# A decoder block on one core: the opening in a new order, scales spread by transposes, first bit chunk high half first

## The reference, cut to what matters

```python
# 1 expert layer: two int8-like "smooth quantised" products with a silu product between
s = sqrt(max|x|, per column / max|w|, per column)
xs, ws = x / s, w * s
x_scale, w_scale = max|xs| per row / 127, max|ws| per row / 127
h = round(xs / x_scale) @ round(ws / w_scale).T * x_scale * w_scale.T
# 2 bit layer: weights rounded to -1, 0, 1 by w / mean|w|
hidden = sigmoid(x @ q(w1).T) * (x @ q(w2).T);  out = hidden @ q(w3).T      # 704 wide
# 3 cross attention: 16 heads over 256 context rows, 8 key/value heads
q = x @ Wq;  k, v = ctx @ Wk, ctx @ Wv;  softmax(q k^T / sqrt(128)) v @ Wo
# 4 gated layer: shared 1024 wide, one routed 128 wide, router over 8
```

## Time and profile before

| what | us |
|---|---|
| median of 3 runs | 419.43 (418.96 to 420.85) |
| the profiled execution | 418.34 |
| its span, first to last instruction | 416.5 |
| PE busy | 398.7 (96%) |
| DVE busy | 300.3 (72%) |
| ACT busy | 229.7 (55%) |
| POOL busy | 163.7 (39%) |

### The profile page before, as it was taken

One profiled execution on the slowest core, in us unless ns is written; L12 is line 12 of the kernel. 1 busy time (PEld: TensorE's weight loads), 2 busy tenths in 40 slices (PEclk: granted clock), 3 DMA queues, 4 the chain that ended last, 5 costly groups with the idle time before them and its releaser, 6 DMA issues.

```text
span 416.5 us, 8853 instructions
## 1 busy us (share of the span) xinstructions
PE 398.7 (96%) x3238; PEld 384.5 (92%) x3238; DVE 300.3 (72%) x942; ACT 229.7 (55%) x636; POOL 163.7 (39%) x261
## 2 busy tenths in 40 slices
PE   8898999999999999999999999999899999999896
PEld 7788899999889999999999999999899989999795
DVE  4788678879766879678667878777757766665644
ACT  1886876656643466566543456566553565655232
POOL 2012764754634233434443334245343233334231
PEclk9999999999999999999999999999999999999999
DMA  7999200000000200000000100000000000000000
GB/s 234 327 343 357 80 0 2 2 2 2 3 0 2 57 23 2 2 0 2 3 25 2 55 0 2 2 2 0 2 27 0 2 2 2 2 2 0 27 2 25
DMA packets 15098, 16.89 MB, mean 41 GB/s; under 512 B 1552, under 2 KB 14032, under 8 KB 15056
## 3 DMA queue, kind: packets, MB, share of 16 engines
q1 hardware_dynamic: 15056, 16.33, 12.2%
HBM read 15.28 MB, written 1.05 MB: 39 GB/s over the span
## 4 chain that ended last, share of the span: by engine, by line
PE 53%; DVE 22%; ACT 12%; POOL 5%; issue 4%; DMA 2%; SPq 1%; DVEq 0%; POOLq 0%
PE bank_s L364 8%; PE bank_qa L364 7%; ACT prob L901 6%; DVE prob L1528 6%; PE bank_pt L364 4%; PE bank_s L554 3%; PE bank_pt L572 3%; PE bank_o L599 3%; PE bank_u L585 3%; DVE pt_lo L1539 3%; DMA w_raw<-in_w3T 2%; DVE ut_lo L1545 2%; PE bank_u L663 2%; PE bank_x L364 2%; PE bank_s L562 2%
## 5 line engine op out<-in xcount | busy, mean ns | idle before, releaser
L1179 POOL TENSOR_SCALAR prob<-prob,row_inv,valid_b 128x256 f32<-128x256 f32 x128 | 70.3, 559 | 100.2 <-DVE row_inv L1535 100.2
L901 ACT ACTIVATE prob<-prob,row_min 128x256 f32<-128x256 f32 x128 | 64.2, 502 | 69.2 <-DVE row_min L1528 69.2
L1539 DVE TENSOR_TENSOR pt_lo<-bank_pt,pt_hi 128x512 fp32r<-128x512 f32 x64 | 44.0, 688 | 17.7 <-ACT pt_hi L861 17.4
L1545 DVE TENSOR_TENSOR ut_lo<-bank_u,ut_hi 128x256 fp32r<-128x256 f32 x64 | 26.9, 420 | 33.3 <-ACT ut_hi L861 32.8
L1528 DVE CUSTOM_DVE_ANT_0 prob<-bank_s,masked 128x256 f32<-128x256 f32 x128 | 48.7, 418 | 2.7 <-PE bank_s L562 1.4
L861 ACT ACTIVATE pt_hi<-bank_pt 128x512 fp32r<-128x512 f32 x64 | 37.5, 586 | 8.8 <-PE bank_pt L572 8.7
L1191 POOL TENSOR_TENSOR act_lo<-act_raw,act_hi 128x256 fp32r<-128x256 f32 x32 | 24.1, 754 | 45.9 <-ACT act_hi L966 45.8
L572 PE MATMUL bank_pt<-ident,prob 128*128 128x128 f32 x256 | 39.1, 275 | 2.0 <-POOL prob L1179 1.7
L364 PE MATMUL bank_qa<-xt_hi,a_hi 128*128 128x256 f32 x126 | 39.5, 314 | 0.1
L364 PE MATMUL bank_qa<-xt_lo,a_hi 128*128 128x256 f32 x126 | 35.2, 279 | 0.0
L599 PE MATMUL bank_o<-c_hi,ut_hi 128*128 128x256 f32 x128 | 34.2, 290 | 1.0 <-ACT ut_hi L861 1.0
(11 more groups left out here) (315 smaller groups left out, 1291.7 us busy)
## 6 DMA issues: line engine op xcount, KB each, us to landing
wq_raw<-in_wqT SPq DMA_DIRECT2D x4, 512.0 KB, 8.9
wo_raw<-in_wo SPq DMA_DIRECT2D x4, 512.0 KB, 8.7
w_raw<-in_w12T SPq DMA_DIRECT2D x2, 704.0 KB, 7.7
gate_raw<-in_gateT SPq DMA_DIRECT2D x2, 576.0 KB, 7.7
up_raw<-in_upT SPq DMA_DIRECT2D x2, 576.0 KB, 9.5
down_raw<-in_downT SPq DMA_DIRECT2D x2, 576.0 KB, 11.4
x<-in_x SPq DMA_DIRECT2D x4, 256.0 KB, 4.6
guT<-in_guT SPq DMA_DIRECT2D x4, 256.0 KB, 3.3
```

Of the source, the lines that this page charges most:

```text
L901: last = act.activation(row, row, ACT.Exp, scale=-1.0, bias=row_min[:, h % 2, t:t + 1], accum_out=row_sum[:, h % 2, t:t + 1])
L1179: last = pool.tensor_scalar(row, row, row_inv[:, h % 2, t:t + 1], valid_b[:, 0:1], ALU.mult, ALU.mult)
L1539: dve.tensor_tensor(pt_lo[:, :, :].rearrange("p s t -> p (s t)"), bank["pt"][:, :], f32(pt_hi[:, :, :].rearrange("p s t -> p (s t)")), ALU ...
L1545: dve.tensor_tensor(ut_lo[:, :], bank["u"][:, 0:T], f32(ut_hi[:, :]), ALU.subtract).then_inc(S["u_l"], 1)
```

## The change

No arithmetic of the result is taken away. The parts:

- **Order of the foldings.** `PREP_ORDER` was 0, 2, 1, 3, 4, 5, ... 15. Now: 0, 2, 1, then all a units (4 to 14), then all c units (3 to 15). Seven foldings of `Wv Wo` so come later; seven units stand before the bit layer instead of eight, two beside it as before, seven behind it instead of six. The loads of `Wq` are issued before those of x and `Wo`.
- **Opening on PE, ACT, DVE** in another order, with fewer transposes of `keep_busy` (141 in place of 156).
- **Spreads** (`q_spread`, `q_spread_weight_scales`) are `pe.transpose` instead of `pe.matmul`, in every batch. The second weight spread of batch 0 goes to bank x1.
- **bit_up** runs all passes with `xt_hi` and then all with `xt_lo`; chunk 0 waits for `lnb_lo` only between them, in every batch. The first queries likewise.
- The first attention head waits for the last folding (`turn_probs`), since unit 15 uses bank pt.
- Three more units of `ffn_weights_hi` and two more of `ffn_weights_lo` are beside the attention heads of batch 0.

```diff
-FFN_HI_HEADS = (2,)
+FFN_HI_HEADS = (0, 1, 2, 4)
-FFN_LO_HEADS = (2, 4, 5, 6, 7, 8)
+FFN_LO_HEADS = (0, 1, 2, 4, 5, 6, 7, 8)
-        PREP_BANKS = ("qa", "o", "s0", "s1", "qa", "o", "x1", "u", "qa", "o", "x1", "o", "s1", "pt", "x1", "o")
+        PREP_BANKS = ("qa", "o", "s0", "qa", "o", "u", "x1", "qa", "o", "x1", "qa", "s1", "pt", "o", "x1", "pt")
-        PREP_ORDER = (0, 2, 1, 3) + tuple(range(4, 2 * PAIRS))
+        PREP_ORDER = (0, 2, 1, 4, 6, 8, 10, 12, 14, 3, 5, 7, 9, 11, 13, 15)
...
-                        last = pe.matmul(dst[:, at + j * P:at + (j + 1) * P], column.to_broadcast([P, P]), ident[:, :],
-                                         start=True, stop=True)
+                        last = pe.transpose(dst[:, at + j * P:at + (j + 1) * P], column.to_broadcast([P, P]),
+                                            ident[:, :])
...
-                    last = pe.matmul(wscale_bank(b)[:, (j - 2) * P:(j - 1) * P],
-                                     qscale[:, s, j:j + 1].to_broadcast([P, P]), ident[:, :], start=True, stop=True)
+                    last = pe.transpose(wscale_bank(b, s)[:, (j - 2) * P:(j - 1) * P],
+                                        qscale[:, s, j:j + 1].to_broadcast([P, P]), ident[:, :])
...
+                for half in (xt_hi, xt_lo):
+                    if c == 0 and half is xt_lo:
+                        pe.wait_ge(S["lnb_lo"], b + 1)
+                    for at, col in sides:
+                        for k in range(ND):
+                            last = pe.matmul(dst[:, at:at + T], w12[:, k, col:col + P], half[:, k, :], start=first,
+                                             stop=(half is xt_lo and k == ND - 1), skip_group_check=True)
...
             def turn_probs(b, h):
                 pe.wait_ge(S["s_norm"], H * b + h + 1)
+                if b == 0 and h == 0:
+                    pe.wait_ge(S["prep_lo"], 16)
...
+            q_bf(0, 0)
             q_wscale(0, 0)
-            q_bf(0, 0)
             ternary12_round(0, 0)
-            prep_hi(0)
             q_tanh(0)
             ternary12_round(0, 1)
+            prep_hi(0)
+            ternary3_round(0)
             prep_hi(1)
...
             q_half_product(0)
-            prep_lo(0)
             q_silu(0)
             ternary12_clip(0, 0)
-            prep_lo(1)
             q_ratio1(0)
-            prep_lo(2)
+            prep_lo(0)
             ternary12_clip(0, 1)
-            prep_lo(3)
             q_scaled_w(0, 1)
...
+            prep_lo(13)
             row_inverses(0, 0)
             queries_lo(0, 1)
             row_inverses(0, 1)
-            q_first_scales(1)
             prep_lo(14)
             prep_lo(15)
+            q_first_scales(1)
```

More of the change, by code:

```diff
@@ L327, in _ @@
             ternary_weights()
-            attention_weights(0)
+            attention_weights("wq", 0)
+            attention_weights("wo", 0)
+            for i in range(1, WQ_LOADS):
+                attention_weights("wq", i)
             mask(0)
             for b in range(1, NB):
-                sp.dma_start(x[:, b, :, :], x_rows(x_in, b)).then_inc(S["x_in"], 16)
+                sp.dma_start(x[:, b, :, :], x_rows(x_in, b)).then_inc(S["x1_in" if b == 1 else "x_in"], 16)
             turned_expert_weights(1)
             for i in range(1, WQ_LOADS):
-                attention_weights(i)
+                attention_weights("wo", i)
             sp.dma_start(router_raw[:, :, :], routerT_in.rearrange("(k p) n -> p k n", p=P)
@@ L476, in bit_up @@
                 first = True
-                for at, col in sides:
-                    for k in range(ND):
-                        w = w12[:, k, col:col + P]
-                        last = split_mm(dst[:, at:at + T], w, None, xt_hi[:, k, :], xt_lo[:, k, :], first, k == ND - 1)
-                        first = False
+                for half in (xt_hi, xt_lo):
[5 more added lines that the diff above has]
+                                             stop=(half is xt_lo and k == ND - 1), skip_group_check=True)
+                            first = False
                 last.then_inc(S["bit_mm"], 1)
@@ L527, in queries @@
                     pe.wait_ge(S["qa_l"], PAIRS * b + p)
+                if b == 0 and h >= 2 and h % 2 == 0:
+                    pe.wait_ge(S["prep_lo"], prep_count(h))
                 dst = bank["qa"][:, (h % 2) * T:(h % 2 + 1) * T]
@@ L535, in first_queries @@
             def first_queries():
-                for k in range(ND):
-                    last = split_mm(bank["u"][:, 0:T], a_hi[:, 0, k, :], a_lo[:, 0, k, :], xt_hi[:, k, :],
-                                    xt_lo[:, k, :], k == 0, k == ND - 1)
+                for n, (w, r) in enumerate(((a_hi, xt_hi), (a_lo, xt_hi), (a_hi, xt_lo))):
+                    if n == 2:
+                        pe.wait_ge(S["lna_lo"], 1)
+                    for k in range(ND):
+                        last = pe.matmul(bank["u"][:, 0:T], w[:, 0, k, :], r[:, k, :], start=(n == 0 and k == 0),
+                                         stop=(n == 2 and k == ND - 1), skip_group_check=True)
                 last.then_inc(S["qa0_mm"], 1)
@@ L593, in project @@
             def project(b, h):
-                if h == 0:
-                    pe.wait_ge(*(S["routed_x"], b) if b > 0 else (S["prep_lo"], 2 * PAIRS))
+                if b == 0 and h == 0:
+                    pe.wait_ge(S["prep_lo"], 2 * PAIRS)
+                elif h == 0:
+                    pe.wait_ge(S["routed_x"], b)
                 pe.wait_ge(S["u_h"], H * b + h + 1)
@@ L803, in _ @@
             prep_unit(0)
+            keep_busy(7, "pt")
+            q_piece(3, 0)
             prep_unit(1)
-            q_piece(3, 0)
+            keep_busy(4, "pt")
+            q_piece(4, 0)
             prep_unit(2)
-            prep_unit(3)
-            keep_busy(8, "pt")
-            q_piece(4, 0)
-            keep_busy(18, "pt")
+            keep_busy(14, "pt")
             q_spread_weight_scales(0, 1)
@@ L849, in _ @@
             prep_unit(15)
-            keep_busy(6, "u")
+            keep_busy(4, "u")
             for b in range(NB - 1):
@@ L1088, in _ @@
[L1088 to L1090 removed]
             ln_hi(0, "lnb", xt_hi)
[L1092 to L1095 removed]
             for c in range(BIT_CHUNKS):
                 bit_sig(0, c)
[L1098 to L1099 removed]
+                if c == 0:
+                    ternary3_done(1)
+                elif c == 1:
+                    ffn_weights_hi(0)
+                elif c == 2:
+                    prep_hi(7)
+                elif c == 3:
+                    ctx_split_hi(0)
+                elif c == 4:
+                    act.wait_ge(S["router_in"], 16)
+                    act.copy(router_hi[:, :, :], router_raw[:, :, :]).then_inc(S["router_hi"], 1)
+                    ffn_weights_hi(1)
@@ L1100, in _ @@
                 bit_high(0, c)
-                if c == 1:
-                    prep_hi(8)
+            prep_hi(8)
+            ffn_weights_hi(2)
             prep_hi(9)
-            for u in range(4, 7):
-                ffn_weights_hi(u)
+            ffn_weights_hi(3)
             prep_hi(10)
             prep_hi(11)
-            ffn_weights_hi(7)
             ln_hi(0, "lna", xt_hi)
@@ L1112, in _ @@
             first_queries_hi()
-            for u in range(8, FFN_HI_EARLY):
+            for u in range(4, 7):
                 ffn_weights_hi(u)
@@ L1119, in _ @@
             prep_hi(15)
+            for u in range(7, FFN_HI_EARLY):
+                ffn_weights_hi(u)
             for b in range(NB - 1):
```

142 lines of the change are left out of this document (68 added, 74 removed).

## The result

| | median us | runs | profiled execution: time, span, granted clock |
|---|---|---|---|
| before | 420.14 | 4 (418.96 to 421.64) | 418.34, 416.5, 1.000 |
| changed | 415.70 | 4 (414.10 to 416.59) | 415.73, 413.7, 0.996 |

A forecast was written before the change was run, and what follows sets the result against it. PE, busy 96% of the span, was taken as the bound, with a chain of small steps in the opening. 3.9 + 2.6 + 1.15 = 7.65 off 418.34 gave 410.7, or 411.8 for the median; range 410.6 to 413, 409.8 to 415.6 with two rivals.

The forecast's parts named there:

- Steps 1 to 4: Opening, first product to the second scale's spread: gain so far 0.25, 1.2, 1.85, then 2.5 us; POOL's power 0.7.
- Step 5: Rounding on POOL, clips now behind: PE's turn at 25.1, gain 2.8 us; second dequantisation at 26.95, gain 2.9.
- Step 6: Norm's power on POOL, DVE's 1280-column clip moved away: 0.70 us in place of 1.28, xn at 30.8, gain 3.45.
- Step 9: Bit layer: same passes, two more idle transposes (0.2 us), residual at 44.75 against 48.72 before, gain 3.95.
- Step 10: First queries: one folding instead of two behind the norm's turn, start at 49.65, gain 4.55 us, then 4.75.
- Step 11: First heads: PE waits 1.0 us for unit 15's low half; second head at 61.2 against 65.10, gain 3.9.
- rival of a longer wait at the first heads: The opening's gain turns into a longer wait there, 2 us more lost: 413.8; chance 0.18.
- The opening, 3.9: Gain in us forecast for the whole new opening, up to the second head of batch 0.
- The spreads, 2.6: Scale spreads as transposes save 0.11 us a call, 10 calls per batch 0 to 2; bounds nothing and 2.9.
- second rival: Spreads and bit_up gain nothing beside attention, since another wait closes after each: 3.9 alone, 415.5; chance 0.12.
- bit_up, 1.15: First bit chunk of batches 1 to 3: high passes fill PE's wait, 0.48 us twice and 0.18.
- Clock: New gaps in the opening costed at nothing; rival, a fall to 1.2 GHz through the bit layer: 422.4, chance 0.03.

The follow-up runs named there:

- experiment 3: Changed kernel with POOL's first two gate_lo moved behind its power of the second norm, DVE's mask left in place: 413.89 us, ratio 0.9833.
- experiment 1: Changed kernel with mask_row(0) moved early, beside bit chunk 3 instead of behind lnq_apply(1) (the early mask): 413.52 us, ratio 0.9856.
- experiment 7: Kernel before with only the spreads as transposes: 418.51 us, ratio 0.9982; kernel before with only bit_up's high half first: 418.76 us, ratio 0.9975.
- experiment 2: Kernel before with mask_row(0) alone moved late, between prep_lo(9) and the bit layer's residual: 424.14 us, ratio 1.0094.

## Why the prediction was wrong, step by step

- **Steps 1 to 4: right** to 0.25 us. Of step 4, POOL's power took 0.98 and not 0.70, since a clip ran beside it, and the steps ahead had been as much too early. **Step 5: 0.5 too much,** nearly all of it the unexplained 0.4 at the dequantisation.
- **Step 6: right.** The row was taken, against the rule that the first starter keeps the ports, and power and clip behaved as the row has them: the power starts first and still ends with the clip (0.98 at 20.65 shows it once more). From variance to xn it is 0.99 in place of 1.57. The step left out that the clip also stood in DVE's own queue ahead of xn, where it alone would have held xn until 34.1, against 34.26. Moving it away took off both, and no run splits them. Here the Trainium skill's rule that the first starter keeps the ports (SBUF — State Buffer, "Who interferes with whom") and the rows differ: a power of two columns does not keep DVE out while it runs.
- **Step 9 failed, and its stall is about half of the whole error.** It reads: "Same passes, two more idle transposes (0.2)." and "The residual, 48.72 before, at 44.75." It came at 48.19. The step costed DVE's queue by durations from the earlier trace rows and never asked what POOL does beside `mask_row(0)` in its new place. The stall is 1.6 to 2.05 us of time (experiments 3 and 1). It was to be had from the trace of before: step 6 had a clip and a power stretched beside each other, and the same thought, turned to a long POOL instruction that comes first, gives this stall. Having found the rule of no use for one pair, I did not apply it to the next. Without the stall the residual is at 46.05, 1.3 late: 0.7 from the first chunk's late start (34.03 in that execution) and 0.6 from the layer itself. PE takes 11.9 for it (34.03 to 45.94, where the foldings follow) and took 11.0 before (37.65 to 48.61); the forecast had allowed 0.4 more than before. 0.2 is the wait for the low half in the first chunk, 0.2 the idle transposes, the rest waits of up to 0.2 ahead of `bit_down`.
- **Step 10 was short of a wait:** four foldings and three idle transposes on PE are as long as the norm's chain, so that even with the early mask the queries start at 51.1 (forecast 49.65).
- **Step 11: right.** Its wait of 1.0 is 1.07, for the same operation, 3.7 us later than forecast. The rival of a longer wait at the first heads (413.8) had the sign and not the place.
- **The opening, 3.9:** measured 0.3 as made, 2.3 at the second head without the stall. So 1.6 of the 3.6 that it fell short are late steps on the way, and 2.0 the stall.
- **The spreads, 2.6:** measured 2.1 to 2.3. The passes after head 0 count next to nothing, which the second rival had for all of them. That rival's 415.5 is 0.2 from the measured median, by luck: it has 3.9 from the opening and nothing from the other two, and measured are 0.3 and 3.6.
- **bit_up, 1.15:** measured 1.5, since batch 1's gives 0.45 and not its wait of 0.18, which understates what PE lost (experiment 7).
- **Clock:** no fall at the new gaps, as forecast. The rival priced one at 10.6 us, the whole bit layer at the lower level. The runs have 1.4 to 1.6: in experiment 2, after 2.69 us of idle PE, the lower level lasted under 4 us.

Together: 0.3 + 2.1 + 1.5 = 3.9 in place of 7.65, beside 4.2 to 5.0 less at equal clock.

## What to carry to other kernels

When an instruction is moved on DVE, look at what POOL runs at its new place, and the other way round: a tensor_scalar of 0.28 us cost 2 us on the path, since it was held by POOL and stood ahead of the one operation that everything waited for. Put such short operations beside idle time of POOL, not behind a phase's last work, where POOL turns to its long background jobs. Read a wait of PE from start to start, not from the bracket alone. And compare kernels by a marker in the middle of the trace and at equal granted clock; with gains of 1 us the medians of a few runs say little.
